# Last layer of a four-layer network: the scaled side output in idle tiles, an opening in another order, and the eighth convolution product ahead of the fifth and sixth gate product

## The reference

```python
k = einsum('btc,dc->btd', x_seq, Wk)            # v the same with Wv
r = sigmoid(einsum('btc,dc->btd', x_seq, Wr))
x_fwd = wkv_scan(real_w, u, k, v)               # and x_bwd on the flipped sequence, flipped back
h = r * (x_fwd + x_bwd) * 0.5
hn = (h - mean(h)) * rsqrt(var(h) + 1e-05) * ln_g + ln_b
out_g = einsum('btc,dc->btd', hn, Wo)
y = conv3x3(x, conv_w) * bn_scale + bn_b
y = where(y > 0, y, 0.01 * y)
return out_g * gamma_g + y * gamma_s
```

## Time and profile before

| what | value |
|---|---|
| median of 3 runs | 4168.81 us (4168.54 to 4170.88) |
| profiled execution, its own time | 4169.36 us |
| span of the profiled execution | 4167.6 us |
| TensorE busy | 3733.4 us, 90% of the span |
| VectorE busy | 2994.8 us, 72% |
| ScalarE busy | 2481.1 us, 60% |
| last layer, from its first instruction to the end | 2859.1 to 4167.6 us |

### The profile page before, as it was taken

How to read it: one execution, slowest core, us unless ns; L and a number is a source line. 1 busy time by engine, 2 the same in 40 slices (tenths; PEclk the granted TensorE clock), 3 DMA queues, 4 the chain that set the end, 5 groups by cost and what they waited for, 6 DMA issues and landing times. The chain is left out here.

```text
span 4167.6 us, 55398 instructions
## 1 busy us (share of the span) xinstructions
PE 3733.4 (90%) x17706; PEld 2429.3 (58%) x17706; DVE 2994.8 (72%) x3031; ACT 2481.1 (60%) x3907; POOL 1436.7 (34%) x1188
## 2 busy tenths in 40 slices
PE   6999999999999999946999995564999999999997
PEld 5777878686868687612555553443555555555553
DVE  4758676767767675558888874256987987887986
ACT  2867777776868686834656644213655655555654
POOL 1857676676757575822112201231000000000000
PEclk8999999999999999967999997886999999999999
DMA  4333434343424343221212123675132132132132
GB/s 128 86 102 102 113 96 119 91 121 87 120 86 122 93 112 87 54 80 35 71 51 66 53 54 111 171 233 203 34 78 72 38 78 72 38 78 72 38 78 47
DMA packets 132957, 372.11 MB, mean 89 GB/s; under 512 B 48162, under 2 KB 49778, under 8 KB 125826
## 3 DMA queue, kind: packets, MB, share of 16 engines
q1 hardware_dynamic: 113858, 298.98, 23.6%
q0 software_dynamic: 17872, 62.55, 7.9%
q10 hardware_dynamic: 1008, 7.67, 0.6%
HBM read 233.79 MB, written 130.60 MB: 87 GB/s over the span
## 5 line engine op out<-in xcount | busy, mean ns | idle before, releaser
L440 POOL TENSOR_TENSOR probs_lo<-probs,probs_hi 128x512 fp32r<-128x512 f32 x848 | 1164.1, 1388 | 588.6 <-ACT probs L487 568.2
L553 DVE TENSOR_REDUCE maxima<-m_psum 128x1 fp32r<-128x1024 f32 x512 | 624.9, 1221 | 369.9 <-PE m_psum L731 369.1
L486 ACT ACTIVATE probs_hi<-s_psum 128x512 fp32r<-128x512 f32 x1024 | 614.0, 600 | 327.1 <-PE o_psum L760 220.0
L2647 PE MATMUL psum<-mixes,last_weights 128*128 128x512 f32 x1728 | 753.6, 594 | 0.0
L487 ACT ACTIVATE probs<-s_psum 128x512 f32<-128x512 f32 x1024 | 608.2, 594 | 0.0
L2647 PEld LDWEIGHTS psum<-mixes,last_weights 128*128 128x128 f32 x1728 | 329.2, 191 | 399.5 <-issue 395.6
L744 PE MATMUL s_psum<-q_all,k_hi 128*128 128x512 f32 x1024 | 430.7, 421 | 26.3 <-ACT probs L487 26.0
L760 PE MATMUL o_psum<-probs_lo,v 128*112 128x512 f32 x1024 | 412.1, 402 | 12.9 <-DVE probs_lo L635 7.9
L745 PE MATMUL s_psum<-q_all,k_lo 128*128 128x512 f32 x1024 | 404.5, 395 | 0.0
L755 PE MATMUL o_psum<-probs_hi,v 128*112 128x512 f32 x1024 | 404.4, 395 | 0.0
L2254 POOL DMA_DIRECT2D out<-side x24 | 20.5, 856 | 1072.1 <-ACT side L2318 1072.1
(11 more groups left out here) (350 smaller groups left out, 6663.8 us busy)
## 6 DMA issues: line engine op xcount, KB each, us to landing
xin<-x SPq DMA_DIRECT2D x17, 1536.0 KB, 7.7
xin<-in_x SPq DMA_DIRECT2D x16, 1536.0 KB, 7.2
k_hi<-k_rows_hi SPq DMA_DIRECT2D x128, 192.0 KB, 3.4
k_rows_hi<-stage_hi SPq DMA_DIRECT2D x48, 256.0 KB, 2.1
k_rows_lo<-stage_lo SPq DMA_DIRECT2D x48, 256.0 KB, 2.3
q_rows_hi<-stage_hi SPq DMA_DIRECT2D x48, 256.0 KB, 2.2
q_rows_lo<-stage_lo SPq DMA_DIRECT2D x48, 256.0 KB, 2.5
k_lo<-k_rows_lo SPq DMA_DIRECT2D x64, 192.0 KB, 4.3
```

The source lines that it names most:

```text
L440: pool.tensor_tensor(probs_lo[:, u % RING, :], probs[:, u % RING, :], as_f32(probs_hi[:, u % RING, :]), ALU.subtract).then_inc(pool_low.ne ...
L486: nc.scalar.activation(probs_hi[:, u % RING, :], s_psum[:, u % 2, :], ACT.Exp, scale=SCALE)
L553: nc.vector.tensor_reduce(maxima[:, g % 2, tile:tile + 1], source, AX.X, ALU.max, negate=True).then_inc(rows_max.next(), 1)
L2647: ins = nc.tensor.matmul(bank, conv_w[:, t, down, factor, m * P:(m + 1) * P], mixes[:, factor, t, down:down + S, :].rearrange("p a b -> p ...
```

## The change

- `RING`: the order "conv 2 to 6, gate 0 to 5, conv 7 to 11" becomes "conv 2 to 6, gate 0 to 3, conv 7, gate 4 and 5, conv 8 to 11". With the ring's six banks, conv 7 now waits for the reading of conv 5, gate 4 for that of conv 6, gate 5 for that of gate 0, and conv 11 for that of conv 7.
- VectorE, item 4: `sum_side(1, 1)` stands ahead of `num_scan` (was behind `both_ways`), `sum_side(1, 2)` behind it (was behind `current`).
- The scaled side tile is written into a tile of its own, `v[:, 0, :]`, `to_e[:, 1, :]` or `to_e[:, 2, :]`; `keep_conv(m)` waits for the scaling before it, no longer for the store; `gap(1)`, `gap(2)` and the multiplication with the gates wait for the stores of these tiles.
- GpSimd issues the three result stores with no wait between them, waits for all three, and frees the three tiles at once.
- Opening: ScalarE's splitting of the weights no longer stands behind the table load and GpSimd's fills; VectorE makes the moments of the first image ahead of the low parts, and the combining of the convolution's weights moves behind `keep_low`, in three operations (one halving goes to ScalarE).

```diff
         RING = run("kv", 0, 6) + run("conv", 0, 1) + run("kv", 6, 10) + run("conv", 1, 2) + run("kv", 10, 12) + run("conv", 2, 7) + \
-            run("gate", 0, 2 * CT) + run("conv", 7, 4 * CT)
+            run("gate", 0, 4) + run("conv", 7, 8) + run("gate", 4, 2 * CT) + run("conv", 8, 4 * CT)
...
-        side_scaled = signal("side_scaled", CT)
-        side_free, out_free = signal("side_free", CT, 1), signal("out_free", CT, CT)
+        side_scaled = signal("side_scaled", CT, 1)
+        side_free, out_free = signal("side_free", CT, CT), signal("out_free", CT, CT)
+        scaled_sides = (v[:, 0, :], to_e[:, 1, :], to_e[:, 2, :])
...
-                    pool.dma_start(target, side[:, :], accum_op=ALU.add).then_inc(side_stored, 16)
+                    pool.dma_start(target, scaled_sides[m], accum_op=ALU.add).then_inc(side_stored, 16)
...
                     pool.dma_start(target, v[:, m, :], accum_op=ALU.add).then_inc(out_stored, 16)
-                    pool.wait_ge(out_stored, 16 * (CT * i + m + 1))
-                    pool.sem_inc(out_free.sem, 1)
+                pool.wait_ge(out_stored, 16 * CT * (i + 1))
+                pool.sem_inc(out_free.sem, CT)
...
-            act.wait_ge(framed.sem, framed.at(11))
-            act.wait_ge(eps_made.sem, 1)
...
-            nc.scalar.preload_act_table_set("natural_log_exp_and_others")
             for name in ("Wk", "Wv", "Wr"):
                 nc.scalar.copy(parts[name, 0], last.lin_w[name]).then_inc(part_high.next(), 1)
+            nc.scalar.preload_act_table_set("natural_log_exp_and_others")
+            act.wait_ge(framed.sem, framed.at(11))
+            act.wait_ge(eps_made.sem, 1)
...
+            middle_taps = conv_w[:, :, :, 1, :]
+            nc.scalar.activation(middle_taps, middle_taps, ACT.Copy, scale=0.5).then_inc(halved.next(), 1)
             act.sem_inc(*out_made.lead())
+            act.sem_inc(*side_scaled.lead())
...
-                    act.wait_ge(side_free.sem, side_free.at(m, i))
+                    act.wait_ge(side_scaled.sem, side_scaled.at(m, i))
...
                     act.wait_ge(side_bent.sem, side_bent.at(m + 1, i))
-                    nc.scalar.activation(side[:, :], side[:, :], ACT.Copy, scale=cols["gamma_s"][:, m:m + 1]).then_inc(side_scaled.next(), 1)
+                    if m == 0:
+                        act.wait_ge(ev_made.sem, ev_made.at(2, i))
+                    nc.scalar.activation(scaled_sides[m], side[:, :], ACT.Copy, scale=cols["gamma_s"][:, m:m + 1]).then_inc(side_scaled.next(), 1)
...
             moments(None)
+            for n, name in enumerate(("Wk", "Wv", "Wr")):
+                dve.wait_ge(part_high.sem, part_high.at(n + 1))
+                nc.vector.tensor_tensor(parts[name, 1], last.lin_w[name], as_f32(parts[name, 0]), ALU.subtract).then_inc(part_low.next(), 1)
             variance(None)
             shift(None)
-            dve.wait_ge(prepared.sem, prepared.at(2))
-            nc.vector.scalar_tensor_tensor(g1, minus, 0.5, g1, ALU.mult, ALU.add).then_inc(prepared.next(), 1)
-            dve.wait_ge(prepared.sem, prepared.at(3))
-            nc.vector.tensor_scalar(minus, minus, 0.5, None, ALU.mult).then_inc(prepared.next(), 1)
+            g0, g1, g2, other = conv_w[:, :, :, 0, :], conv_w[:, :, :, 1, :], conv_w[:, :, :, 3, :], conv_w[:, :, :, 2, :]
+            nc.vector.tensor_tensor(other, g0, g2, ALU.add).then_inc(prepared.next(), 1)
+            dve.wait_ge(framed.sem, framed.at(11))
             dve.wait_ge(parts_stored, 16 * 7)
             for n in range(4):
                 mix(n, None)
             keep_low(None)
+            dve.wait_ge(prepared.sem, prepared.at(1))
+            dve.wait_ge(halved.sem, halved.at(1))
+            nc.vector.scalar_tensor_tensor(g1, other, 0.5, g1, ALU.mult, ALU.add).then_inc(prepared.next(), 1)
+            dve.wait_ge(prepared.sem, prepared.at(2))
+            nc.vector.tensor_tensor(other, other, g1, ALU.subtract).then_inc(prepared.next(), 1)
...
                     dve.wait_ge(max_made.sem, max_made.at(n + 1, i))
+                    if n in (1, 2):
+                        dve.wait_ge(side_free.sem, side_free.at(n + 1 - CT, i))
...
                         quotient(n - 1)
+                    if n == 4:
+                        sum_side(1, 1)
                     num_scan(n)
+                    if n == 4:
+                        sum_side(1, 2)
...
                 dve.wait_ge(h_made.sem, h_made.at(ITEMS, i))
+                dve.wait_ge(side_free.sem, side_free.at(1, i))
```

More of the change, by code:

```diff
@@ L2134, in rwkv_layer @@
         xin_free = signal("xin_free3")
+        halved = signal("halved")
         framed = signal("framed")
@@ L2405, in _ @@
         def _(dve):
[L2406 to L2413, removed]
             def moments(i):
@@ L2570, in _ @@
                         bend(0)
-                    if n == 4:
-                        sum_side(1, 1)
                     current(n)
@@ L2581, in _ @@
                         shift(i)
-                    if n == 4:
-                        sum_side(1, 2)
                 quotient(ITEMS - 1)
@@ L2641, in fill @@
                         if n == 0:
-                            pe.wait_ge(prepared.sem, 4)
+                            pe.wait_ge(prepared.sem, 3)
                         if m == 0:
```

## The result

The changed kernel takes 4204.71 us (median of 4 runs, 4203.44 to 4208.81) beside 4169.16 before: a ratio of 1.0087, 95% interval 1.0074 to 1.0099. It is slower by 0.87%; 4209 was forecast. The profiled execution took 4203.44 us, its span is 4201.7 (4167.6 before). Lines of the changed kernel have other numbers: the Wo product is L2702, convolution products L2654, kv and gate products L2672, the copies of k and v L2308.

What follows compares the result with a forecast made beforehand. TensorE bounds the kernel: 149.8 us of work per pass, some 6 us to win. Seven passes at +7.25 (50.7), first pass +2.0, opening -5.8, end -6.5: +40.4 on 4169.36, 4209 us; range 4168 to 4240.

Steps and rivals of the forecast that it cites:

- The new order: Convolution product 7 ahead of gates 4 and 5: hole moves ahead of the means; pass 158.0 us with the clock, +2.0.
- The wait for the third store: ScalarE's copy of k/v product 2 waits until 3540.9; `exps(0)` 8.35 us late, a pass of 163.2 us, +7.25.
- TensorE's other waits up to there ... lie inside this one: TensorE's waits for product 1 read and group moments lie inside the delay of convolution product 7 to 3618.05.
- The rule on shared engines: Transfers of all engines share the same 16 DMA engines and interleave; the 14.17 us store wait was said to agree.
- the rival of early landings: Stores land in under 10 us, only the hole moves: 4172 us, or 4161 with the clock up; chance 0.16.
- Opening and end: Opening: first product 5.8 us sooner (0 to 8); end: last stores save 6.5 us (3 to 8); each once.
- The side tile: Scaled side in tiles of its own: takes the 6.36 us store wait from ScalarE; new waits cost 0.

Runs made afterwards that it cites:

- the last run above: Changed kernel with the old ring order and result stores in series, each tile freed as it lands, except the last image's: 4119.24 us, ratio 0.9877, a pass of 150.7.
- the held store: Changed kernel with the second result store held until the low part of Wv has landed, three tiles freed together: 4240.96 us, ratio 1.0163, a pass of 166.1.
- the best version: Changed kernel with the old ring order and stores in series, freed one by one, except the last image's: 4119.24 us, ratio 0.9877.

## Why the prediction was right, step by step

**The new order** was priced right: a hole ahead of the means, 158.0 us a pass with the clock; without the new stores the changed kernel takes 157.9. Gate 5 to the means took 21.8 us (3642.9 to 3664.68), 21.67 were read from the trace of before. The +2.0 us over before are the order and the two moved reads together: beside the last run above, which has these reads and the old order (150.7), the new order costs 7.2 us a pass.

**The wait for the third store** was named with its place and its price per us. Its length was a little too high: the store was put at 16.2 us behind Wo (3540.9 - 3524.67), and in the pass shown the copy of kv product 2, which waits for it, starts 14.9 us behind Wo (3550.84 - 3535.98). So `exps(0)` is 6.8 us late instead of 8.35 (15.8 less 9.0). A pass came to 162.5 instead of 163.2.

**One step failed**, though the time hides it: "TensorE's other waits up to there ... lie inside this one". The load of Wv was not followed past the stores that now run beside it. It makes TensorE wait 1.5 to 4.2 us at product 2 in every one of the seven passes. In two of them (4.19 and 3.83 us, a granted clock of 0.50 behind both) it sets the end instead of the stores: these passes take 164.6 and 164.3 us, where the pass from 3197.22 to 3358.00, with a wait of 1.56, took 160.8. The prediction has TensorE wait 5.2 us in all up to product 7 (3612.84 to 3618.05). In five passes the wait for the load does lie inside that, and leaves 0.2 to 1.9 us of it at product 7 (1.50 and 1.93 in the pass from 3358.00); in the two with the long waits none is left there, and the slowed matmuls come on top (who waited for whom: us, times, longest; 3100 to 4150):

```profile
PE psum L2672 <- DMA lin_slot<-Wv_part: 15.4, 6, 4.2
...
PE psum L2654 <- DVEq L2549: 6.3, 5, 1.9
```

That the mean pass comes so near to the forecast is partly luck. The five passes with the store in the chain take 161.7 us in the mean, about the forecast's 163.2 less the 1.5 us by which `exps(0)` was put too late; the two with the load, 164.4, bring the mean up to 162.5.

The two causes lie side by side, on VectorE's route and TensorE's: freeing each tile on its own leaves 161.2, the wait alone at its length here would give about 162 (166.1 less the 4.1 us by which the held store's wait is longer). To take back the stores' cost both have to go.

**The rule on shared engines.** The traces show how the stores and SyncE's transfers meet (DMA queues in 3538 to 3540 and in 3542 to 3544 of the changed kernel: packets, MB, time as a share of 16 engines):

```profile
q0 software_dynamic: 61, 0.19, 48.5%
q1 hardware_dynamic: 63, 0.29, 46.2%
...
q1 hardware_dynamic: 19, 0.75, 93.5%
q0 software_dynamic: 20, 0.08, 21.4%
```

Packets go one to one in both stretches. In the first, 61 packets of the second store stand among the load's 63, and the load lands after 8.3 us instead of 3.8. (A store has 144 packets, as the side store's in 3520 to 3531; from 3531 to 3542 queue q0 counts 288, two stores, so the third's begin behind 3542.) In the second, 20 packets of about 4 KB stand among 19 of about 39 KB, and the third store moves 0.08 of the 0.83 MB. The Trainium skill, "DMA: Bandwidth & Descriptors", section "Queues, rings and completion order", says that an engine goes round the queues packet by packet; the traces agree, with these counts. The Trainium skill's price for a transfer from GpSimd (same page, section "Anatomy of one DMA — SWDGE (gpsimd) path"), about 2.0 us and 436 KB per us, is not seen here: no result store landed in under 5.2 us in any run. That price would have given the rival of early landings.

**Opening and end.** From the layer's first instruction to its first product it was 40.44 us before (2859.13 to 2899.57) and 34.21 after (timelines of SyncE and TensorE):

```profile
2856.10 0.36 SPq L2206 DMA_DIRECT2D xin<-x  x1
...
2890.31 2.92 PE L2672 MATMUL psum<-xp_hi,lin_slot 128*128 128x512 f32 x6 [21.74 <-DVE xp_lo L2437]
```

That is 6.2 us, 5.8 were forecast. The end, from Wo's last product (4188.61) to the span's, takes 13.1 us where it took 18.5: 5.4 us, 6.5 forecast.

```profile
4189.62 0.86 POOL L2262 DMA_DIRECT2D out<-v  x1 [3.55 <-ACT v L2404]
```

**The side tile** cost nothing that shows, as forecast: the best version has it, with TensorE idle for 0.4 us in a pass; no run took it alone. It isn't what most of the gain needs either: the two reads alone bring 34 of the 52 us between before and the best version, with ScalarE still waiting for the side tile's store.

## What to carry to other kernels

Filling a hole of one engine is worth nothing if the work that fills it was the cover of a wait further on: read how long the chain behind each product is, put the products with the longest chain first, and fill the hole by bringing forward what it waits for (here two short reads). When several transfers are issued at once and freed together, whoever needs the first waits for the last, and a transfer of another queue that was just in time can come late: follow every consumer of every queue, also those that the edit doesn't touch. Two causes on two routes hide each other, so take each away alone and both together before one is called the cause.

## What the hardware showed that was not expected

A wait of TensorE can cost more than its length, and even a short one can: in the run with the new order alone, a wait of 2.50 us was followed by a product of 9.66 us instead of 7.89, at a granted clock of 0.50. The length of the wait alone does not tell. Ahead of kv product 2 of the changed kernel six matmuls took 2.15 us after a wait of 1.73 (granted clock 0.67 in 3057 to 3060), and 1.65, as usual, after one of 2.82 (1.00 in 3868.5 to 3871); what makes the difference these runs do not show (timeline of TensorE):

```profile
3057.01 2.15 PE L2672 MATMUL psum<-xp_hi,lin_slot 128*128 128x512 f32 x6 [1.73 <-DMA lin_slot<-Wv_part]
...
3868.47 1.65 PE L2672 MATMUL psum<-xp_hi,lin_slot 128*128 128x512 f32 x6 [2.82 <-DMA lin_slot<-Wv_part]
```

A load of 0.59 MB that landed in 3.7 to 4.1 us before took 5.6 to 8.3 with the second and third store of 0.5 MB in flight, and 3.7 to 4.0 again when these two were held back until it had landed.
